# Half of the first slot's query and key loads moved from SyncE's DMA queue to ScalarE's

## The reference, cut to what matters

```python
x = x + 0.5 * _L0_ffn_ref(_layernorm(x), ...)
x = x + _L0_attn_ref(_layernorm(x), ...)
x = x + 0.5 * _L0_ffn_ref(_layernorm(x), ...)
```

```python
qkv = (x @ qkv_w.T + qkv_b).reshape(B, T, 3, H, dh)      # B=4, T=1024, H=16, dh=8
scores = jnp.einsum('bhtd,bhsd->bhts', q, k) * scale
attn = jax.nn.softmax(jnp.where(causal, -jnp.inf, scores), axis=-1)
seq_out = jnp.einsum('bhts,bhsd->bhtd', attn, v)
```

## Time and profile before

| | us |
|---|---|
| median of 3 runs | 1978.31 |
| lowest, highest | 1975.79, 1980.07 |
| the profiled execution, its own time | 1976.37 |
| its span in the trace | 1974.6 |
| PE busy | 1906.1 (97%) |
| VectorE busy | 1624.1 (82%) |
| ScalarE busy | 1481.9 (75%) |
| GpSimd busy | 915.7 (46%) |

### The profile page before, as it was taken

How to read it: one execution, slowest core, us unless ns; L and a number is a source line. 1 busy time by engine, 2 the same in 40 slices (tenths; PEclk the granted TensorE clock), 3 DMA queues, 4 the chain that set the end, 5 groups by cost and what they waited for, 6 DMA issues and landing times. The chain is left out here.

```text
span 1974.6 us, 52910 instructions
## 1 busy us (share of the span) xinstructions
PE 1906.1 (97%) x18490; PEld 1131.0 (57%) x18490; DVE 1624.1 (82%) x5453; ACT 1481.9 (75%) x4089; POOL 915.7 (46%) x549
## 2 busy tenths in 40 slices
PE   7999999999999989999999999899999999999997
PEld 4777763577775343434434367437777646777743
DVE  7999964899994479999999769779999548999844
ACT  5999993799996253777777754469999837999952
POOL 2788860588881040000000046337878406787700
PEclk9999999999999986999999999999999999999999
DMA  6222220122220040111111000002212201222301
GB/s 188 44 47 46 46 60 6 35 46 45 46 62 23 6 152 28 41 42 42 43 42 43 18 5 2 2 21 47 48 43 47 55 6 42 44 47 45 68 10 43
DMA packets 76106, 85.08 MB, mean 43 GB/s; under 512 B 17139, under 2 KB 50499, under 8 KB 75715
## 3 DMA queue, kind: packets, MB, share of 16 engines
q1 hardware_dynamic: 75551, 81.67, 16.7%
q10 hardware_dynamic: 292, 0.03, 0.0%
HBM read 21.14 MB, written 8.39 MB: 15 GB/s over the span
## 5 line engine op out<-in xcount | busy, mean ns | idle before, releaser
L304 ACT ACTIVATE probs<-probs,negmax 128x128 f32<-128x128 f32 x1024 | 399.8, 396 | 24.0 <-DVE negmax L377 23.2
L2069 ACT ACTIVATE gprobs<-ps_global 128x1024 f32<-128x1024 f32 (+3 forms) x384 | 291.4, 811 | 128.8 <-PE ps_global L1539 106.2
L259 POOL TENSOR_TENSOR rot<-rot 128x1024 f32<-128x1024 f32 x128 | 302.3, 2362 | 141.4 <-DVE rot L347 141.4
L265 POOL TENSOR_TENSOR qk<-rot,cnorm 128x1024 f32<-128x1024 f32 x128 | 243.7, 1904 | 119.2 <-POOL rot L259 90.4
L272 POOL TENSOR_TENSOR probs<-probs,iden 128x1024 f32<-128x1024 f32 x128 | 242.8, 1897 | 120.2 <-DVE iden L385 120.2
L1766 DVE TENSOR_REDUCE maxes<-ps_global 128x1 f32<-128x512 f32 (+2 forms) x384 | 222.1, 637 | 11.3 <-PE ps_global L1502 7.1
L377 DVE CUSTOM_DVE_ANT_0 probs<-ps_attn,masks 128x128 f32<-128x128 f32 x1024 | 225.7, 283 | 0.1
L1497 PE MATMUL ps_global<-kq 48*128 48x512 bf16 (+3 forms) x768 | 198.0, 347 | 11.7 <-DMA kq<-split_scratch 5.7
L304 ACT ACTIVATION_READ_ACCUMULATOR probs<-probs,negmax 128x1 f32 x1024 | 197.0, 192 | 0.0
L345 DVE TENSOR_TENSOR rot<-ps_attn,rotary 128x512 f32<-128x512 f32 x256 | 174.7, 682 | 2.1 <-PE ps_attn L171 1.6
L1999 POOL CAST m_parts<-m_turn 32x128 bf16<-32x128 f32 x16 | 4.5, 280 | 367.7 <-DVE m_turn L1780 367.7
(11 more groups left out here) (206 smaller groups left out, 4583.1 us busy)
## 6 DMA issues: line engine op xcount, KB each, us to landing
v_first<-v_second SPq DMA_DIRECT2D x256, 128.0 KB, 2.3
hs<-z_a SPq DMA_DIRECT2D x256, 32.0 KB, 1.9
ln<-z_b SPq DMA_DIRECT2D x56, 128.0 KB, 2.3
kq<-split_scratch SPq DMA_DIRECT2D x64, 96.0 KB
kq<-split_scratch SPq DMA_DIRECT2D x64, 64.0 KB
split_scratch<-parts SPq DMA_DIRECT2D x8, 384.0 KB, 3.7
split_scratch<-gprobs SPq DMA_DIRECT2D x8, 384.0 KB, 4.5
x_tok<-in_x_dram SPq DMA_DIRECT2D x4, 512.0 KB, 6.5
```

The lines of the kernel that those rows point to most:

```text
L259: nc.gpsimd.tensor_tensor(a, a, b, ALU.add).then_inc(C["rot_sum"], 1)
L265: nc.gpsimd.tensor_tensor(qk[:, k % 2, :].rearrange("p (h d) -> p h d", d=DH), rot_a[:, k % 2, :, :], cnorm[:, k % 2, :].unsqueeze(2).to_b ...
L304: last = nc.scalar.activation(probs[:, k % 2, slot, :], probs[:, k % 2, slot, :], ACT.Exp, scale=-1.0, bias=negmax[:, k % 2, slot:slot + 1 ...
L2069: nc.scalar.activation(probs[:, step % RING, 2 * p:2 * p + 2, 0:w], ps[:, S0 + 2 * p:S0 + 2 * p + 2, 0:w], ACT.Exp).then_inc(C["p2_exp"], 1)
```

## The change

The second half of slot 0's load is no longer issued by SyncE between write 3 and write 4. ScalarE issues the same six DMAs from its own queue, two each after `copy_values` of chunks 3, 4 and 5. Before the first of them ScalarE waits for the writes of chunks 0 and 1 and for the memsets of the tile (`pj_ones`). Sources, destinations, sizes and the semaphore `qk_in0` stay the same. In the order of issue they are: queries one part, queries two parts; queries three parts, keys one part; keys two parts, keys three parts.

```diff
+FIRST_LOADS = (3, 4, 5)
...
+            def load_second_half(i):
+                which, (first, end) = i // len(JOINED), JOINED[i % len(JOINED)]
+                if i == 0:
+                    for m in range(2):
+                        act.wait_ge(C[f"pj_written{m}"], C.after(f"pj_written{m}", written_count(m)))
+                    act.wait_ge(C["pj_ones"], C.after("pj_ones", 2))
+                row = 64 + AD * sum(e - f for f, e in JOINED[0:i % len(JOINED)])
+                stored = scratch[which, 0, PARTS - end:PARTS, 0, 1] if which else scratch[which, 0, 0:end, 0, 1]
+                act.dma_start((ks if which else qs)[0][row:row + AD * end, :, :].rearrange("k p t -> k (p t)"),
+                              stored.rearrange("j d p t -> j d (p t)")).then_inc(C["qk_in0"], 16)
...
                 copy_values(m)
+                if m in FIRST_LOADS:
+                    load_second_half(2 * FIRST_LOADS.index(m))
+                    load_second_half(2 * FIRST_LOADS.index(m) + 1)
...
             write(2)
             load(0, (0,))
             write(3)
-            load(0, (1,))
             for m in range(4, CHUNKS):
                 write(m)
             load(1)
```

## The result

| | kernel before | changed kernel |
|---|---|---|
| median of 12 runs, us | 1978.41 | 1982.16 |
| lowest, highest | 1975.79, 1980.07 | 1977.68, 1983.69 |
| profiled execution, own time | 1976.37 | 1982.65 |

The ratio is 1.0018 with a 95% interval of 1.0010 to 1.0025: the change made the kernel slower by 2 to 5 us, 3.7 by the medians. That is inside the 0.2% for which the forecast had "the same", and on its slow side.

The account below looks back on a forecast made before the run. It took VectorE as the bound from the first maximum on: write 3 late by 2.2 us, less 0.68 us of slack, loses 1.5 us, giving 1979.8 us on the median of 1978.31; range 1975.6 to 1983.5.

Parts of the forecast that it names:

- Who is last: Before VectorE's first maximum, the load of `kq` is last by only 0.68 us; VectorE's chain covers 5.04 of 5.72 us.
- The first rival: Write 3 is not held up; the load's wait goes, VectorE's chain stays, 0.7 us gained, 1977.6 us; chance 0.2.
- Write 3 behind the moved bytes: On the three load-carrying DMA engines, second and third pairs delay write 3 by 2.2 us, between 0 and 3.9.
- the holes: Some 2 us of idle on the three engines during first half and write 3, to absorb part of the moved bytes.
- The second branch of my 2.2: Write 3's delay if the third pair alone (160 KB) goes ahead of it on the three engines: 2.2 us.
- The sum: At the seam, `high_part` of chunk 7 moves to 725.7, first maximum from 729.69 to 731.2: a loss of 1.5 us.
- the unknown term: How much of the second half is served ahead of write 3: 0 to 3.9 us, giving 1977.6 to 1981.5 us.
- VectorE's chain, 5.5 us: VectorE's work from the start of ScalarE's `high_part` of chunk 7 to the memset's end takes 5.5 us.
- ScalarE's issue time at no cost: Three pairs push ScalarE back by 2.3 us at most, inside the 2.31 us it waits for write 3: cost 0.
- The rival that makes ScalarE's queue the bound: Held-up issues make ScalarE late at chunk 7; 5.3 us slower, 1983.6; decides above 4.1 us for six issues; chance 0.13.
- SyncE's 4.05 us at no worth: Six issues leave SyncE's queue, so writes 4 to 7 and slot 1's load can go earlier; costed at 0.
- the rival in which it holds: TensorE keeps 2.4 GHz because the fills start early enough; 4.2 us faster, 1974.1 us; chance 0.07.

Follow-up runs that it names:

- the two memset runs: VectorE's memset moved from its chain's end to before the last split_low, in the changed kernel (ratio 1.0014) and in the kernel before (0.9998).
- the second profile: Profile of the changed kernel run once more, unedited; ratio 1.0016 against the kernel before.
- third_pair_late: Changed kernel with the third pair of loads (160 KB) issued after chunk 6 and not after chunk 5; ratio 1.0001 against the kernel before.
- one_part_both_queues: Changed kernel with each load DMA cut into DMAs of one part, second half still on ScalarE's queue; ratio 1.0004 against the kernel before.

## Why the prediction was right, point by point

- **Who is last.** Right, and now shown by the two memset runs: the load by less than 0.7 us in the kernel before, VectorE's chain in the changed one. The first rival's point, that the prize of 5.7 us was covered but for 0.68, held: the first fill came 2.9 us earlier (35.14 to 32.21) and bought nothing.
- **Write 3 behind the moved bytes.** Right in kind, too small. I gave 2.2 us between 0 and 3.9; `high_part` of chunk 7 was 3.5 us late (3.7 in the second profile). The mis-sized term is the holes: I let them swallow 2.0 us of the 3.9 us of bytes, and they swallowed about 3.9 - 3.5 = 0.4. Moving the third pair was worth 2.3 us, near the 2.2 of its size. How the remaining 1.2 us divide is not shown. The second branch of my 2.2, the third pair alone, thus had the right number for that pair and left out the rest. The prediction weighed two orders of service. The Trainium skill, page DMA: Bandwidth & Descriptors, section Queues, rings and completion order, has each DMA engine take turns among the queues; `third_pair_late` agrees with that (2.3 us), and speaks against service in the order of issue.
- **The sum.** 1.5 us in the seam became 2.7, inside the bounds of 0.7 faster and 3.2 slower, and 3.7 in the timed median. The measured 1982.16 is 0.7 us above 1981.5, where the unknown term alone would have ended; it is in the range only by the 2 us added for the spread of the runs. The 1 us beyond the seam was no part of the forecast, so that part of the hit is luck.
- **VectorE's chain, 5.5 us.** Right: 38.67 - 33.23 = 5.44 us from `high_part` to the first maximum, which follows the memset at once.
- **ScalarE's issue time at no cost.** Right: 0.32 to 0.76 us each, chunk 6 late by 0.63, and TensorE not at all. The six took 3.6 us against the limit of 4.1, and the margin was wider still, since each pair overlaps with the copy in front of it. The rival that makes ScalarE's queue the bound did not come true in the change, but it did in `one_part_both_queues`.
- **SyncE's 4.05 us at no worth.** Right, for another reason than given. I let writes 4 to 7 and slot 1's load be issued earlier. The first five of the eight issues were, the first by 721.23 - (719.48 - 2.40) = 4.1 us and the next four by 0.1 to 1.7; the last three came 2.4 to 2.9 us later. What held them was the parts that they store. The second DMA of write 4 went out at 722.6, when VectorE ended chunk 4's low part (721.49 + 1.04 = 722.53), and the last three at 732.2 to 734.3, behind the late chunk 7, each issued in 0.36 us. So the delay of write 3 came back to SyncE, and slot 1's load was issued from 734.81 - 2.40 = 732.4, 1.4 us later than before, with six issues fewer in front. No wait of 1 us or more hangs on it. VectorE's low part of chunk 4, and the issues of single writes (ns min/median/max, first and last start):

```profile
721.49 1.04 DVE L1754 TENSOR_TENSOR parts<-gprobs,parts 128x512 bf16<-128x512 f32 x1
...
L2235 SPq DMA_DIRECT2D split_scratch<-parts x2: 360/1420/2479, 722.6 to 723.0; - x2
...
L2235 SPq DMA_DIRECT2D split_scratch<-gprobs x3: 359/360/360, 732.2 to 734.3; - x3
```

- **The clock.** It fell as before, and that ruled out the rival in which it holds: the fills started at full clock (0.21 us for the first, against 0.26), but with VectorE late TensorE idled 5.96 us.

## What to carry to other kernels

Before a transfer is brought forward, ask what else the DMA engines move in that time, and whether an earlier wait hangs on it: here a load that nobody could use yet held up a write that the longer chain was waiting for. The share of DMA time while one kind of transfer runs alone hints at how wide it is; 0.21 of sixteen is the worth of about three engines. In this seam cutting such DMAs brought the first maximum to 33.63 us, further than any other queue or order (34.98 at best), though the timed ratio shows the gain only together with the moved memset. A wait of 5.7 us is worth only what lies between it and the next one to arrive, and a small edit in that next chain (the memset) tells which of the two is last.

## What the runs showed of the hardware that I had not expected

- A second queue is not neutral for order: 160 KB on ScalarE's queue, issued 1.0 to 2.4 us after write 3, held that write up by 2.3 us. In the first maximum, moving the half there lost 2.7 us or gained 2.7 us, by what stood behind the loads.
- The issue of a DMA can take several times its usual time, on either queue: a write of 384 KB that is issued in 0.36 to 0.49 us took 2.48 us in the changed kernel and 2.67 in the kernel before, and five small loads on ScalarE's queue took 3.3 us, of which ScalarE's work behind them paid 2.46. That many outstanding DMAs are the cause is a guess.
- A DMA of one part takes 4.20 / 12 = 0.35 us to issue where the mixed ones take 3.77 / 6 = 0.63 us: twice the number of DMAs cost 0.4 us more in all.
